# Relation adjacency built with one matmul a pair into two double banks, copied in turn by ScalarE and VectorE

## The chip, the cores and the metric

One core of a Trainium2 chip runs the kernel. The metric is the device time in microseconds of one execution. TensorE (PE), VectorE (DVE), ScalarE (ACT), GpSimd (POOL) and SyncE (SP) each take their own instructions in order and meet only at semaphores.

## The reference

A graph has 6250 nodes with 128 features and 206,250 edges sorted by destination. A SAGE network of two layers and a layer norm come first. Then come three relational convolutions. For each node d, relation r (5 of them) and layer:

```
agg[d, r] = mean of h[src] over the edges (src -> d) of relation r     (0 if there are none)
out[d]    = sum over r of agg[d, r] @ W[r]  +  h[d] @ root + bias
```

The first takes 256 inputs (128 features and a learned row for one of 3 node types) to 256, the second 256 to 128, the third 128 to 128; each ends in a ReLU. The result is added to the input of the three and normalised.

## The kernel before

**The first part (SAGE)** ends near 1488 us and is not touched, nor is its code.

**The relational convolutions** are `conv_sync`, `conv_pool`, `conv_tensor`, `conv_scalar` and `conv_vector`, one for each engine. A class `Plan` lays all of them out in half ticks. An even half tick begins with a *group*: 512 edges. POOL gathers their source rows with four indirect DMAs into one of six slots of `messages` (L1395); DVE makes one-hot columns of the destinations four groups ahead (L1669); PE multiplies rows by one-hots into one of two banks (L1408, and L1412 for the node types in the first convolution); DVE adds the bank into a ring of sums (L1690, L1691). POOL may fill a slot again when the group that used it is through PE (`group_psum`).

**Windows.** When the edges of 256 nodes (a *window*) are summed, a finish of twelve half-tick steps runs among the groups. In the first convolution: step 0, DVE scales the sums by the inverse counts (L1730), clears them (L1737) and marks node types (L1766), and SP moves the scaled type rows together with small DMAs (L1305). Step 1, PE makes the window's 256 outputs in two halves (L1495, L1496, L1493 and L1497; the last two need the DMAs' rows) into bank 4. Step 2, ACT applies bias and ReLU (L1601). Step 3, PE makes the root product of the second convolution into bank 5 (L1502) and right behind it the table product of the first 128 nodes into banks 6 and 7 (L1473). Step 4, ACT copies the root product (L1605) and the first piece of the table rows (L1582); step 5, DVE makes the residue (L1747); step 6, PE makes the second table product, which waits for that residue, and ACT and DVE go on with the pieces (L1586, L1752) to step 10. There are 25 windows.

**Building.** The second and third convolutions take the edges into the last 2688 nodes from dense matrices, source by destination, one for each relation. They are built during the first convolution: 1344 pairs of destination nodes, two pairs a *couple*, a couple each half tick, 672 couples in 20 windows. DVE makes, four pairs at a time, a one-hot of the source's lane (L1678, 128 columns) and one of the source's tile, node and relation (L1679, 490 columns). `build` (L1416) has PE multiply them for each pair. The 490 columns are cut in two slices, of 25 and 24 source tiles; slice 0 of both pairs goes to bank 2 and slice 1 to bank 3, 4 matmuls a couple. `evict` (L1548) copies them as fp8 into `stage`: ACT copies slice 0 (L1558), DVE slice 1 (L1560), of every couple. PE waits before each slice for the copy of the couple before. Eight couples fill a stage; two stages take turns, and ACT sends each to HBM with two DMAs (L1572). ACT's copy comes first in its half tick; DVE's copy of a couple comes first in the half tick after, before the one-hots of a later group, the add of a group and the scaling of a window.

The dense matmuls (L1450) of the later convolutions use banks 2 and 3 and wait at their start for the last copies.

Of the kernel before, what the change touches and what calls it, by code (L numbers as in the profile page):

```python
# [5 lines left out]
P = 128  # L6
# [4 lines left out]
RELATIONS = 5  # L11
# [165 lines left out]
def resnorm_gnn(nc, a, out):  # L177
# [27 lines left out]
    with ctx:  # L205
        sem = lambda name: ctx.enter_context(nc.semaphore(name))
        bank = [ctx.enter_context(nc.psum_tensor(f"bank{n}", [P, 512], f32)) for n in range(8)]
# [1000 lines left out]
        rel_evicted = [sem(f"rel_evicted{n}") for n in range(SLICES)]  # L1208
# [8 lines left out]
        REL_BANKS, PART_BANKS = DENSE_BANKS, TABLE_BANKS  # L1217
# [17 lines left out]
        def conv_sync(sp):  # L1235
# [62 lines left out]
            for w in range(WINDOWS_1):  # L1298
# [13 lines left out]
                if w == WINDOWS_1 - 3:  # L1312

                    sp.wait_ge(rel_hot_made, REL_BATCHES)
                    sp.wait_ge(rel_psum, COUPLES * SLICES)
# [82 lines left out]
        def conv_tensor(pe):  # L1398
# [17 lines left out]
            def build(j):  # L1416

                b, m = divmod(2 * j, BATCH)
                if m == 0:
                    pe.wait_ge(rel_hot_made, b + 1)  # L1420
                for n in range(SLICES):
                    if j:
                        pe.wait_ge(rel_evicted[n], j)
                    of_part = slice(2 * SLICE_FIRST[n], 2 * (SLICE_FIRST[n] + SLICE_TILES[n]))
                    width = 2 * SLICE_TILES[n] * RELATIONS
                    for q in range(2):
                        hot = rel_hot[:, b % 2, m + q, :].rearrange("p (r c) -> p r c", r=RELATIONS)[:, :, of_part]
                        mm = pe.matmul(bank[REL_BANKS[n]][:, q * width:(q + 1) * width], lo_dense_hot[:, b % 2, m + q, :], hot, start=True, stop=True)  # L1428
                    mm.then_inc(rel_psum, 1)

            def dense(v, step):
# [8 lines left out]
                if at == 0:  # L1440
                    if K >= 2:
                        pe.wait_ge(dense_kept, K - 1)
                    else:
                        pe.wait_ge(rel_evicted[K], COUPLES)
# [21 lines left out]
            def table(w, t):  # L1466
                n = w * WINDOW_TILES + t
                pe.wait_ge(wide_made, w + 1)
                pe.wait_ge(rest_made, ROW_SPLITS + n)
                nodes = slice(t * P, (t + 1) * P)  # L1470
                for b, cols in enumerate((slice(0, FIRST_CUT), slice(FIRST_CUT, RELATIONS * FEAT))):
                    for half in range(2):
                        mm = pe.matmul(bank[TABLE_BANKS[b]][:, 0:cols.stop - cols.start], h_wide[:, half, nodes], w2[:, half, cols], start=(half == 0), stop=(half == 1))  # L1473
                mm.then_inc(table_psum, 1)

            def finish(v, i, n):
# [4 lines left out]
                if v == 0:  # L1481
                    if n == 1:
# [3 lines left out]
                        pe.wait_ge(wide_made, w)  # L1486
                        to = [bank[WIDE_BANK][:, half * WINDOW:half * WINDOW + cols] for half in range(2)]
# [10 lines left out]
                    if n == 3:  # L1498
                        pe.wait_ge(wide_made, w + 1)
                        pe.wait_ge(root_kept, w)  # L1500
# [684 lines left out]
```

## Time and profile before

| | us |
|---|---|
| median of 3 runs | 6984.27 |
| lowest, highest | 6974.2, 6988.96 |
| profiled execution, span from first to last instruction | 7027.7 |
| PE busy, of the span | 4925.6 (70%) |
| POOL busy | 3636.8 (52%) |
| DVE busy | 2875.6 (41%) |
| ACT busy | 1023.1 (15%) |

The profiled execution has no time of its own beside its span. A line of the profile names the engine, the line of the code, the operation, what is written and read, and how often. "Idle before" is the time in which the engine stood still ahead of it, with what ended it. Starts of PE's matmuls are when they were issued; their ends are modelled. The granted clock is PE's, 1.0 for 2.4 GHz and 0.5 for 1.2 GHz.

### The profile page before, as it was taken

The numbers are of one execution on the slowest core, as the hardware profiler recorded it, in microseconds if no ns is written. First come the engines' busy times: TensorE is split into PE (matmuls) and PEld (weight loads), VectorE is DVE, ScalarE is ACT, GpSimd is POOL, SyncE is SP. The second block draws the span as 40 slices with busy tenths as digits, with TensorE's granted clock in tenths as the row PEclk, the third lists the DMA queues.
The fourth block names the chain that finished last, engine by engine and source line by source line (L and its number), as shares of the span: only waits on it lengthen the run. The fifth ranks groups of instructions, "written<-read, shape, count | busy, mean of one in ns | idle before, by whom it ended". The sixth has DMA issues, their size and how long they took to land.

```text
span 7027.7 us, 95103 instructions
## 1 busy us (share of the span) xinstructions
PE 4925.6 (70%) x35932; PEld 3076.0 (44%) x35932; DVE 2875.6 (41%) x8139; ACT 1023.1 (15%) x2385; POOL 3636.8 (52%) x3575
## 2 busy tenths in 40 slices
PE   2776789955655655656554448888888788888887
PEld 1544556633333333333333334444444445544544
DVE  5766661136666666666662211111112212111212
ACT  2544440002222222212220000000000000000000
POOL 4000000036666666666666646666666566666664
PEclk6888889977777777777776669999999899999999
DMA  2222216543434434434343334554545444444443
GB/s 77 96 111 100 90 64 227 219 135 113 121 106 120 120 105 122 119 112 117 114 116 97 97 116 134 168 167 148 169 137 167 154 138 146 138 139 147 142 135 104
DMA packets 428468, 904.12 MB, mean 129 GB/s; under 512 B 71170, under 2 KB 335116, under 8 KB 406124
## 3 DMA queue, kind: packets, MB, share of 16 engines
q0 software_dynamic: 169216, 348.44, 18.4%
q1 hardware_dynamic: 129028, 454.04, 17.7%
q10 hardware_dynamic: 129768, 95.53, 4.3%
q8 instruction: 289, 4.73, 0.3%
q14 instruction: 167, 1.37, 0.1%
HBM read 692.22 MB, written 205.05 MB: 128 GB/s over the span
## 4 chain that ended last, share of the span: by engine, by line
PE 43%; another core or an unknown queue 15%; issue 9%; DVE 8%; ACT 2%; DVEq 1%; DMA 0%; SPq 0%; ACTq 0%; POOL 0%; POOLq 0%
PE bank L1450 23%; PE bank L1408 7%; PE bank L1428 5%; PE bank L1495 2%; PE bank L1473 2%; PE bank L1412 2%; ACT stage L1558 1%; DVE stage L1560 1%; DVE scaled L1730 1%; DVE rel_hot L1679 1%; DVE type_scaled L1730 1%; DVE lo_dense_hot L1678 1%; DVE sums L1691 1%; DVE sums L1737 1%
## 5 line engine op out<-in xcount | busy, mean ns | idle before, releaser
L1395 POOL DMA_INDIRECT messages<-table,src_rows x2552 | 2653.3, 1040 | 1384.9 <-issue 692.0
L1450 PE MATMUL bank<-slices,pieces 128*128 128x384 fp8e4 x10290 | 1978.4, 337 | 375.5 <-issue 361.2
L1450 PEld LDWEIGHTS bank<-slices,pieces 128*128 128x128 bf16 x10290 | 988.8, 100 | 1211.6 <-issue 704.5
L1428 PE MATMUL bank<-rel_hot,lo_dense_hot 128*128 128x240 bf16 (+1 forms) x2688 | 589.2, 331 | 914.5 <-ACT stage L1558 463.2
L1395 POOL DMA_INDIRECT messages<-table,rel_rows x940 | 899.5, 957 | 560.8 <-issue 250.7
L1691 DVE TENSOR_TENSOR sums<-sums,bank 128x120 f32 x873 | 236.4, 271 | 2292.1 <-remote 1826.1
L1408 PE MATMUL bank<-group_hot,messages 128*128 128x120 bf16 x10476 | 832.5, 239 | 238.8 <-issue 112.8
L1408 PEld LDWEIGHTS bank<-group_hot,messages 128*128 128x128 bf16 x10476 | 747.4, 111 | 357.1 <-issue 204.8
L1428 PEld LDWEIGHTS bank<-rel_hot,lo_dense_hot 128*128 128x128 bf16 x2688 | 193.0, 106 | 1243.6 <-ACT stage L1558 532.2
L1377 POOL IOTA iota_rel_i<- 128x490 int32 x1 | 1.4, 1394 | 1355.2 <-DMA table<-typed_rows 1355.2
L1558 ACT CAST stage<-bank 128x500 fp8e4<-128x500 f32 x672 | 387.2, 576 | 1772.5 <-PE bank L1428 1094.9
L1560 DVE CAST stage<-bank 128x480 fp8e4<-128x480 f32 x672 | 435.0, 647 | 242.7 <-PE bank L1428 219.4
L877 PE MATMUL bank<-adjacency,x_pieces 128*128 128x384 bf16 (+1 forms) x2499 | 485.2, 336 | 0.0
L1679 DVE TENSOR_SCALAR rel_hot<-iota_rel,rel_dense 128x490 bf16<-128x490 f16 x1344 | 468.5, 349 | 0.0
L975 ACT CAST adjacency<-bank 128x400 bf16<-128x400 f32 x784 | 392.0, 504 | 440.4 <-PE bank L853 434.4
L1690 DVE TENSOR_TENSOR type_sums<-type_sums,bank 3x120 f32 x403 | 107.1, 266 | 812.0 <-remote 591.9
L853 PE MATMUL bank<-q_hot,lo_hot 128*128 128x100 bf16 x3136 | 230.9, 222 | 267.5 <-DVE rd_hot L1057 258.8
L877 PE MATMUL bank<-adjacency,h_pieces 128*128 128x384 bf16 (+1 forms) x2499 | 398.9, 320 | 0.0
L1678 DVE TENSOR_SCALAR lo_dense_hot<-iota,lo_dense 128x128 bf16<-128x128 f16 x1344 | 354.9, 264 | 0.0
L1669 DVE TENSOR_TENSOR group_hot<-iota,group_code 128x480 bf16<-128x480 f16 x873 | 349.5, 401 | 1.6
L853 PEld LDWEIGHTS bank<-q_hot,lo_hot 128*128 128x128 bf16 x3136 | 193.1, 105 | 344.3 <-DVE rd_hot L1057 258.7
L877 PEld LDWEIGHTS bank<-adjacency,h_pieces 128*128 128x128 bf16 x2499 | 238.5, 98 | 151.8 <-issue 3.8
(251 smaller groups left out, 3593.3 us busy)
## 6 DMA issues: line engine op xcount, KB each, us to landing
slices<-relations_d SPq DMA_DIRECT2D x70, 1200.0 KB
slices<-relations_d SPq DMA_DIRECT2D x70, 1152.0 KB
adjacency_d<-adjacency SPq DMA_DIRECT2D x15, 4704.0 KB, 14.5
adjacency<-adjacency_d SPq DMA_DIRECT2D x15, 4704.0 KB, 15.0
relations_d<-stage ACTq DMA_DIRECT2D x84, 500.0 KB
messages<-table,src_rows POOLq DMA_INDIRECT x2552
relations_d<-stage ACTq DMA_DIRECT2D x84, 480.0 KB
inverse<-inverse_d SPq DMA_DIRECT2D x52, 640.0 KB
```

The lines of the kernel that those rows point to most:

```text
L853: mm = pe.matmul(to[:, m * PAIR_COLS:(m + 1) * PAIR_COLS], lo_hot[:, i % 2, pair, :], q_hot[:, i % 2, pair, :], start=True, stop=True)
L877: mm = pe.matmul(bank[SUM_BANKS[k % 2]][:, 0:cols], pieces[:, h, piece, :], adjacency[HALF[c]][:, h, 0:cols], start=(m == 0), stop=(m == N ...
L975: act.copy(to, pairs).then_inc(evicted, 1)
L1395: pool.indirect_dma_start(messages[:, i % MESSAGES, t, 0:ROWS[v]], None, GATHERED[v], bass.IndirectOffsetOnAxis(ap=rows[:, e:e + 1], axis= ...
L1408: mm = pe.matmul(to[:, 0:GROUP_COLS], messages[:, i % MESSAGES, t, piece * P:(piece + 1) * P], group_hot[:, i % MESSAGES, t, :], start=(t ...
L1428: mm = pe.matmul(bank[REL_BANKS[n]][:, q * width:(q + 1) * width], lo_dense_hot[:, b % 2, m + q, :], hot, start=True, stop=True)
L1450: mm = pe.matmul(bank[DENSE_BANKS[K % 2]][:, 0:CHUNK], pieces[M % PIECE_RING][:, tile % PIECE_TILES, piece * P:(piece + 1) * P], slice_of_ ...
L1558: engine.copy(to, from_bank, saturate=False).then_inc(rel_evicted[n], 1)
L1560: engine.tensor_copy(to, from_bank, saturate=False).then_inc(rel_evicted[n], 1)
L1669: vec.tensor_tensor(group_hot[:, i % MESSAGES, :, :].rearrange("p k (c t) -> p k c t", t=2), iota16[:, 0:GROUP_COLS].rearrange("p (c t) -> ...
L1678: vec.tensor_scalar(lo_dense_hot[:, b % 2, m, :], iota16[:, :], lo_dense[:, b * BATCH + m:b * BATCH + m + 1], None, ALU.is_equal)
L1679: op = vec.tensor_scalar(rel_hot[:, b % 2, m, :], iota_rel[:, :], rel_dense[:, b * BATCH + m:b * BATCH + m + 1], None, ALU.is_equal)
```

## The change

- One matmul a pair now makes all 490 columns. The two pairs of a couple go to the two banks of `couple_banks[j % 2]`: banks 2 and 3 for even couples, 4 and 5 for odd ones. PE waits for the copy of the couple two before.
- A copy takes a whole couple, 980 columns out of two banks: ACT copies the even couples, DVE the odd ones. `rel_evicted` counts per engine.
- The order of the 490 columns follows the slices already in the one-hot (two iotas in place of one).
- The window product (`WIDE_1`) moves to bank 6, the root product to the first half of bank 6, the table product to bank 7 and the second half of bank 6. So the first table product moves from step 3 to step 4 and waits for ACT's copy of the root product; the window product waits for the last copies and residues of the window before.
- Waits of SP, DVE, ACT and of the first dense product follow the new counters.

```diff
-        bank = [ctx.enter_context(nc.psum_tensor(f"bank{n}", [P, 512], f32)) for n in range(8)]
+        low_banks = [ctx.enter_context(nc.psum_tensor(f"bank{n}", [P, 512], f32)) for n in range(2)]
+        couple_banks = [ctx.enter_context(nc.psum_tensor(f"couple_bank{n}", [P, 2, 512], f32)) for n in range(2)]
+        high_banks = [ctx.enter_context(nc.psum_tensor(f"bank{n}", [P, 512], f32)) for n in range(6, 8)]
+        bank = low_banks + [pair[:, n, :] for pair in couple_banks for n in range(2)] + high_banks
...
+        WIDE_1, ROOT_1 = bank[6][:, 0:2 * WINDOW], bank[6][:, 0:WINDOW]
+        TABLES_1 = (bank[7][:, 0:3 * P], bank[6][:, WINDOW:WINDOW + 2 * P])
...
-            pool.iota(iota_rel_i[:, :], [[P // 2, RELATIONS], [1, NODE_TILES], [512, 2]], base=0, channel_multiplier=0).then_inc(iota_rel_made, 1)
+            for n in range(SLICES):
+                first, width = 2 * RELATIONS * SLICE_FIRST[n], 2 * RELATIONS * SLICE_TILES[n]
+                pool.iota(iota_rel_i[:, first:first + width], [[P // 2, RELATIONS], [1, SLICE_TILES[n]], [512, 2]],
+                          base=SLICE_FIRST[n], channel_multiplier=0).then_inc(iota_rel_made, 1)
...
-                for n in range(SLICES):
-                    if j:
-                        pe.wait_ge(rel_evicted[n], j)
-                    of_part = slice(2 * SLICE_FIRST[n], 2 * (SLICE_FIRST[n] + SLICE_TILES[n]))
-                    width = 2 * SLICE_TILES[n] * RELATIONS
-                    for q in range(2):
-                        hot = rel_hot[:, b % 2, m + q, :].rearrange("p (r c) -> p r c", r=RELATIONS)[:, :, of_part]
-                        mm = pe.matmul(bank[REL_BANKS[n]][:, q * width:(q + 1) * width], lo_dense_hot[:, b % 2, m + q, :], hot, start=True, stop=True)
-                    mm.then_inc(rel_psum, 1)
+                if j >= 2:
+                    pe.wait_ge(rel_evicted[j % 2], j // 2)
+                for q in range(2):
+                    mm = pe.matmul(couple_banks[j % 2][:, q, 0:REL_COLS], lo_dense_hot[:, b % 2, m + q, :], rel_hot[:, b % 2, m + q, :], start=True, stop=True)
+                mm.then_inc(rel_psum, 1)
...
+                pe.wait_ge(root_kept, w + 1)
...
-                        pe.wait_ge(wide_made, w)
+                        pe.wait_ge(root_kept, w)
+                        pe.wait_ge(rest_made, ROW_SPLITS + w * WINDOW_TILES)
...
                         mm.then_inc(root_psum, 1)
+                    if n == 4:
                         table(w, 0)
...
-        def evict(engine, n, j):
+        def evict(engine, j):
...
-            engine.wait_ge(rel_psum, j * SLICES + n + 1)
-            if m == 0 and u >= 2:
+            engine.wait_ge(rel_psum, j + 1)
+            if m < 2 and u >= 2:
...
+            from_banks = couple_banks[j % 2][:, :, 0:REL_COLS].rearrange("p q (c d) -> p c q d", d=2)
+            to = stage[:, u % 2, :, 4 * m:4 * m + 4].rearrange("p c (q d) -> p c q d", q=2)
+            if j % 2 == 0:
+                engine.copy(to, from_banks, saturate=False).then_inc(rel_evicted[0], 1)
             else:
+                engine.tensor_copy(to, from_banks, saturate=False).then_inc(rel_evicted[1], 1)
...
-                        if 0 <= j < COUPLES:
-                            evict(act, 0, j)
+                        if 0 <= j < COUPLES and j % 2 == 0:
+                            evict(act, j)
...
-                    if v == 0 and 0 <= couple_at(half - 1) < COUPLES:
-                        evict(vec, 1, couple_at(half - 1))
+                    if v == 0 and 0 <= couple_at(half - 1) < COUPLES and couple_at(half - 1) % 2 == 1:
+                        evict(vec, couple_at(half - 1))
```

## Rows read from the trace of the kernel before

**Rows 1.** The page, part 4: shares of the chain that ended last.
```profile
PE 43%; another core or an unknown queue 15%; issue 9%; DVE 8%; ACT 2%; DVEq 1%; DMA 0%; SPq 0%; ACTq 0%; POOL 0%; POOLq 0%
```

**Rows 2.** Stretches: from:to, length, busy us (instructions) by engine, clock, DMA share, GB/s.
```profile
1488.00:3724.00 2236.00, 1302.37 (x9117) 821.95 (x9118) 1451.63 (x4643) 458.69 (x852) 1507.66 (x1381) 0.74 0.41 116
3724.00:4142.00 418.00, 176.36 (x1213) 130.10 (x1212) 102.19 (x254) 19.54 (x42) 231.18 (x232) 0.64 0.29 82
```

**Rows 3.** Waits of POOL, 1488 to 3724 us: total us, times, longest.
```profile
POOL messages L1395 <- issue: 377.5, 1236, 0.5
POOL messages L1395 <- PE bank L1412: 203.3, 64, 9.2
POOL messages L1395 <- remote: 147.6, 81, 4.4
```

**Rows 4.** Groups by form, 1488 to 3724 us: count | busy us, mean ns | idle before.
```profile
L1560 DVE CAST stage<-bank 128x480 fp8e4<-128x480 f32 x672 | 435.0, 647 | 242.7 <-PE bank L1428 219.4 <-remote 14.1 <-issue 8.7
L1558 ACT CAST stage<-bank 128x500 fp8e4<-128x500 f32 x672 | 387.2, 576 | 1772.5 <-PE bank L1428 1094.9 <-remote 632.2 <-issue 34.9
L1586 ACT CAST table_rows<-rest_w 128x640 bf16<-128x640 f32 x40 | 29.1, 728 | 3.8 <-issue 3.8
L1605 ACT ACTIVATE root_part<-bank,bias 128x256 f32<-128x256 f32 x20 | 9.6, 479 | 0.0
```

**Rows 5.** Time line, head of a window: start us, length us, engine, line, operation.
```profile
2500.43 2.37 DVE L1730 TENSOR_TENSOR scaled<-sums,inverse 128x1280 f32<-128x1280 f32 x1
...
2508.88 0.58 PE L1428 MATMUL bank<-rel_hot,lo_dense_hot 128*128 128x240 bf16 x2 [8.67 <-DVE stage L1560]
...
2514.52 0.69 PE L1493 MATMUL bank<-type_scaled,emb 18*128 18x256 f32 x2
...
2515.15 2.42 PE L1495 MATMUL bank<-scaled,w 128*128 128x256 f32 x10
...
2518.56 0.60 PE L1428 MATMUL bank<-rel_hot,lo_dense_hot 128*128 128x250 bf16 x4
...
2520.37 0.94 POOL L1395 DMA_INDIRECT messages<-table,src_rows  x1 [6.66 <-PE bank L1412]
```

**Rows 6.** Time line, tail of the same window.
```profile
2526.67 0.87 DVE L1747 TENSOR_TENSOR rest_w<-bank,table_rows 128x384 f32<-128x384 f32 x2
...
2528.16 0.58 PE L1428 MATMUL bank<-rel_hot,lo_dense_hot 128*128 128x240 bf16 x2 [0.92 <-DVE stage L1560]
...
2533.59 0.94 POOL L1395 DMA_INDIRECT messages<-table,src_rows  x1 [2.10 <-PE bank L1412]
```

**Rows 7.** Time line, head of a window with no builds in it.
```profile
3881.36 2.48 DVE L1730 TENSOR_TENSOR scaled<-sums,inverse 128x1280 f32<-128x1280 f32 x1
...
3895.07 1.21 PE L1493 MATMUL bank<-type_scaled,emb 18*128 18x256 f32 x2 [4.07 <-DMA type_scaled<-node_hot]
...
3896.21 4.45 PE L1495 MATMUL bank<-scaled,w 128*128 128x256 f32 x10
...
3903.03 0.94 POOL L1395 DMA_INDIRECT messages<-table,src_rows  x1 [4.75 <-PE bank L1412]
```

**Rows 8.** Time line, catch-up of the window of rows 5.
```profile
2563.19 0.57 ACT L1558 CAST stage<-bank 128x500 fp8e4<-128x500 f32 x1 [7.62 <-remote]
...
2563.38 0.95 POOL L1395 DMA_INDIRECT messages<-table,src_rows  x1 [1.87 <-remote]
...
2581.14 0.95 POOL L1395 DMA_INDIRECT messages<-table,src_rows  x1 [1.80 <-remote]
```

**Rows 9.** Stretches from one window's scaling to the next, with and without builds.
```profile
2610.38:2715.87 105.49, 60.70 (x434) 38.45 (x434) 69.48 (x225) 21.98 (x41) 71.71 (x66) 0.76 0.41 116
...
3881.40:3985.30 103.90, 41.65 (x304) 30.91 (x304) 23.65 (x63) 4.27 (x9) 68.08 (x68) 0.63 0.31 82
```

**Rows 10.** Stretches: second half of the window product, with and without builds.
```profile
2514.50:2518.60 4.10, 4.10 (x18) 2.82 (x18) 0.00 (x0) 0.00 (x0) 0.00 (x0) 1.00 0.06 17
...
3895.10:3900.30 5.20, 5.20 (x12) 3.74 (x13) 0.00 (x0) 0.00 (x0) 2.56 (x3) 0.50 0.30 76
```

More of the change, by code:

```diff
@@ L1442, in dense @@
                         pe.wait_ge(dense_kept, K - 1)
-                    else:
-                        pe.wait_ge(rel_evicted[K], COUPLES)
+                    elif K == 0:
+                        for n in range(2):
+                            pe.wait_ge(rel_evicted[n], COUPLES // 2)
                 if within == 0 and piece == 0:
@@ L1472, in table @@
                     for half in range(2):
-                        mm = pe.matmul(bank[TABLE_BANKS[b]][:, 0:cols.stop - cols.start], h_wide[:, half, nodes], w2[:, half, cols], start=(half == 0), stop=(half == 1))
+                        mm = pe.matmul(TABLES_1[b], h_wide[:, half, nodes], w2[:, half, cols], start=(half == 0), stop=(half == 1))
                 mm.then_inc(table_psum, 1)
@@ L1485, in finish @@
                             pe.wait_ge(emb_in, 16 * (RELATIONS + 1))
-                        pe.wait_ge(wide_made, w)
-                        to = [bank[WIDE_BANK][:, half * WINDOW:half * WINDOW + cols] for half in range(2)]
+                        pe.wait_ge(root_kept, w)
+                        pe.wait_ge(rest_made, ROW_SPLITS + w * WINDOW_TILES)
+                        to = [WIDE_1[:, half * WINDOW:half * WINDOW + cols] for half in range(2)]
                         f_cols = [slice(half * P, (half + 1) * P) for half in range(2)]
@@ L1581, in row_pieces @@
                     for b, at_r, count in ((0, 0, 3), (1, 3, 2)):
-                        op = act.copy(rows[:, at_r:at_r + count, 0, :], bank[TABLE_BANKS[b]][:, 0:count * P].rearrange("p (r f) -> p r f", f=P))
+                        op = act.copy(rows[:, at_r:at_r + count, 0, :], TABLES_1[b].rearrange("p (r f) -> p r f", f=P))
                     op.then_inc(high_made, 1)
@@ L1600, in finish @@
                         for half in range(2):
-                            op = act.activation(h_wide[:, half, 0:cols], bank[WIDE_BANK][:, half * WINDOW:half * WINDOW + cols], ACT.Relu, bias=bias[:, 2 + half:3 + half])
+                            op = act.activation(h_wide[:, half, 0:cols], WIDE_1[:, half * WINDOW:half * WINDOW + cols], ACT.Relu, bias=bias[:, 2 + half:3 + half])
                         op.then_inc(wide_made, 1)
@@ L1604, in finish @@
                         act.wait_ge(root_psum, w + 1)
-                        act.activation(root_part[:, nodes], bank[ROOT_BANK][:, 0:cols], ACT.Identity, bias=bias[:, 4:5]).then_inc(root_kept, 1)
+                        act.activation(root_part[:, nodes], ROOT_1[:, 0:cols], ACT.Identity, bias=bias[:, 4:5]).then_inc(root_kept, 1)
                         row_pieces(w, 0, 0)
```

25 lines of the change are left out of this document (9 added, 16 removed).

## The prediction

> **What bounds the kernel now.** I read the stretches first, then the waits of the gathering engine, then the time line of one window of nodes. Three relational convolutions follow a first part that ends near 1488 us. The change touches the first of them (1488 to 4142 us) and, within it, above all the 2236 us in which the dense relation matrices are built [rows 2]. PE is busy for 1302 of these 2236 us, DVE for 1452, POOL for 1508, ACT for 459 [rows 2]; no engine is full. What ends the waits is the ring of six message groups between POOL and PE. POOL issues 1381 gathers of 1507.66/1381 = 1.09 us each, and the gap that it always leaves between two of them is 377.5/1236 = 0.31 us [rows 3]; the rest of its idle time, 203.3 + 147.6 us less 145 such gaps, about 306 us, is a full ring: POOL waits for the group matmuls of PE [rows 3]. The chain of waits shows it too: PE holds 43% and an unnamed releaser 15% [rows 1]. So a us that PE saves counts only where POOL's ring is full, and at most 306 us are there to be had in this stage.
>
> Where the ring is full is seen in one window (256 nodes, 16.5 groups by the plan, about 105 us [rows 9]). Head: DVE starts to scale at 2500.43, PE is held by DVE until 2508.88, does the fp32 matmuls of the window, waits once more for a small DMA until 2514.52, and POOL gets its first free slot at 2520.37 after 6.66 us idle [rows 5]. Tail: to about 2545, POOL has gaps of its own; the one at 2533.59 is 2.10 us [rows 6]. Catch-up: for the other 60 us a cycle of 17.8 us repeats in which POOL issues 12 gathers (three groups), fills the ring, and PE, DVE, ACT and POOL resume together; ACT and POOL show it at 2563.19 and 2563.38, and the next cycle starts at 2581.14 [rows 8]. The releaser there is "remote": PE had issued its matmuls long before, and the profile doesn't say what held their marks back.
>
> The best row for this change is a stretch without any building: after 3724 us such a window takes 103.9 us, against 105.5 us with the building in it [rows 9]. It also has other DMAs, but it says that the builds are almost hidden today. POOL's mean gather there is 231.18/232 = 1.00 us against 1.09 [rows 2]: of the difference between stages a good part is DVE's one-hots slowing POOL, and those stay.
>
> **The change part by part.** Counts: 672 couples, two of them a group, in 20 windows; 5 more windows have no builds.
>
> Build matmuls: four of 250 or 240 columns (and four weight loads) become two of 490. The columns streamed are the same 980. A row of four at full clock spans 0.60 us [rows 5], latency of the last included. Two weight loads fewer save nothing if they overlap and at most 2 x 0.1 us a couple, 0.4 us of PE a group, 134 us in 336 groups; hidden behind POOL's 5 us a group (4 x 1.25) except in head and tail. I take 0 here and count it in the tail.
>
> Evictions: ACT copies 500 elements in 576 ns and DVE 480 in 647 ns for each couple [rows 4]; after it each takes 980 elements of every second couple. ACT has also 640 elements in 728 ns, a slope of (728 - 576)/140 = 1.09 ns an element; so 728 + 340 x 1.09 = 1.10 us for 980 on ACT, and 647 + 500 x 1.09 = 1.19 us on DVE. Bounds: DVE in proportion, 647 x 980/480 = 1.32 us; below, no cheaper than 0.9 us. A group costs DVE 1.19 instead of 2 x 0.647 = 1.29 us, minus 0.1 us x 336 = -34 us of DVE time, ACT 1.10 instead of 1.15. Neither is on the path in the catch-up. At the head one eviction stood right before the scaling and is now ACT's: -0.65 us a window (0 to -0.65), x 20 = -13 us. What stands between the source's two banks costs nothing in my sum; were it 0.3 us a copy, DVE would be where it is now.
> The Trainium skill says (VectorE: DVE Perf Modes, "The TRN2 errata") that VectorE and ScalarE pay a fixed part per instruction, once for a large one: by its table 980 elements from PSUM are an estimated 1.15 us on VectorE and 0.96 us on ScalarE. The sum would be within 10 us of mine.
>
> Two sets of banks, head: PE's build no longer waits for the eviction that DVE makes after its scaling. PE waited 8.67 us for it [rows 5]. Now PE can start the window's matmuls when the scaling is done, near 2505, some 4 us sooner. But the second half of these needs type rows that go through a DMA after DVE's scaling, 14.1 us after the scaling began (2514.52 - 2500.43), 13.7 in the window without builds (3895.07 - 3881.36) [rows 5, 7]. So what is late next is that DMA: the gain is its remaining wait, about 0.4 us. And there is a price. With builds, PE runs from 2508.88 into the wait, hardly pauses, and the second half has clock 1.00: ten matmuls in 2.42 us [rows 5, 10]. Without builds PE starts early, stands still for 4.07 us, and the second half has 0.50: the same ten take 4.45 us [rows 7, 10]. From scaling to POOL's first free slot it is 19.9 us with and 21.7 us without builds [rows 5, 7]. I take +2.0 us for the lost clock in nine windows out of ten, less 0.4: +1.4 us x 20 = +28 us; bounds -0.4 (the clock holds) to +2.5.
>
> Two sets, tail: PE waits in its builds for DVE (0.92 us at 2528.16 [rows 6]) and again at three more builds before 2545. They go, and POOL's gaps there shrink. Floor: in the tail POOL waits beyond its usual gaps for about 3.4 us; all of it gone is -3.4, and nothing gained 0. The second table product needs DVE's residue (0.87 us from 2526.67 [rows 6]) in any case, and that is ready only about 1 us before it is used today. I take -1.5 us x 20 = -30 us.
>
> Shared bank: the root product, its copy by ACT (0.48 us [rows 4]), then the table product, where it used to follow directly; one build now stands between, about 0.45 us, and covers most. ACT's copy is behind its eviction of the even couple (1.10 us), which has the root product's 1.0 us as cover. Behind PE's wait stand a table product, the next group and POOL. 0.1 to 0.8 us; I take 0.3 x 25 windows = +8 us. The window product's new waits are for things done 60 us earlier: 0.
>
> Catch-up: three groups in 17.8 us, 5.93 us a group, of which 4 x (0.95 + 0.30) = 5.0 is POOL's own [rows 8]. With two sets PE can issue one build and one group more before it blocks. If this makes a cycle of four groups with today's gap of 1.87 us, it is 5.5 to 5.8 us; if the gap grows as it does without builds, no gain or 0.2 us loss. About 11 groups a window x 20 = 220 groups: bounds -90 to +45 us. No row decides; I take 0.
>
> The stage stores wait for both counters and for the same eight couples: 0. DVE can now also wait for a store (second couple of a stage), but ACT's waits are at full rings and not for stores: 0. Two iotas instead of one, before the first gather: under 1 us. In the later convolutions only the first dense product's wait changes: 0.
>
> Sum: -13 + 28 - 30 + 8 + 0 = -7 us on a profiled span of 7027.7 us, which is 43 us (0.6%) above the median of the runs, 6984.3; the terms are carried over as they are, and rounded: 6980 us.
>
> **Rivals.** (a) The clock. The head's loss is full and the tail gives little: +2.5 x 20 = +50, -0.5 x 20 = -10, shared bank +0.5 x 25 = +12, DVE -13, say +40 us: 7024 us. For it: all windows without builds have the slow second half. Against: PE has a build and a group just before. It decides from the point where the head's +1.9 us is more than eviction and tail bring (2.15 us a window).
> The Trainium skill (TensorE: Matmul & The Clock Gate, "HAM oscillation") speaks against this change with the same rule: an array left idle is throttled to half its clock and what follows starts cold. The rows on the second half agree with it (1.00 against 0.50).
> (b) The ring gains. Run-ahead makes cycles of four groups, clock or not: 220 x -0.25 = -55, tail -40, +10 for the rest: 6984 - 85 = 6900 us. For it: PE and ACT wait for each other's single set in every active cycle. Against: these cycles end with POOL's ring, not with PE's work, and 103.9 us without any build is no better than this.
> (c) The change doesn't do what it says: copies across two banks take 1.32 us or more and PE waits for DVE as before, with a build that now needs a whole couple copied. DVE is busy 1452 of 2236 us; 0.3 us x 336 = 100 us more of it, a third of it seen: 7015 us.
>
> **How the numbers follow.** My case (gain and loss cancel) 0.36, the clock 0.26, the ring 0.28, the copies 0.10. A run tells about 0.2%, 14 us, from no change. My case reaches from 6955 to 7000 us: 0.08 of it faster by more, 0.28 same. So faster 0.08 + 0.28 = 0.36, same 0.28 + 0.02 = 0.30, slower 0.24 + 0.10 = 0.34. The range for 8 in 10 goes from the ring's case to the clock's with some of their own spread: 6890 to 7035; my own case's range is 6955 to 7000.
>
> **What would show it.** Right: DVE copies of 128x980 near 1.19 us, ACT's near 1.10; PE's wait for DVE's eviction at the head gone and a wait for the type rows of some 4 us there; granted clock 0.5 in the second half of the window matmuls; POOL's first free slot 20 to 22 us after the scaling; stage length 2236 us within 30. Wrong: second halves at 1.00 (then -30 to -50 us more), cycles of other than 12 gathers, POOL's waits for PE's groups far from 350 us, a mean gather that leaves 1.09 us.

## The result and the profile after

The changed kernel takes 6933.88 us (median of 8 runs, 6914.56 to 6947.71), the kernel before, beside it, 6975.67 us (8 runs, 6953.44 to 6988.96): ratio 0.9941, 95% interval 0.9929 to 0.9953, 42 us or 0.6% faster. The time lies in my range, but that range is wide enough to hold the times of all three rivals too; my likeliest case was no measurable change (6980 us), and it came out on the side of rival (b).

The profiled execution of after has a span of 6929.0 us. Its page, first the busy time, then the chain of waits (answers to [rows 1]), then groups of instructions:

```profile
PE 4825.4 (70%) x34588; PEld 2947.4 (43%) x34588; DVE 2832.1 (41%) x7803; ACT 972.3 (14%) x2049; POOL 3715.9 (54%) x3576
...
PE 34%; another core or an unknown queue 14%; DVE 14%; issue 10%; DVEq 1%; SPq 1%; DMA 1%; POOL 1%; ACT 1%; ACTq 0%; POOLq 0%
...
L1432 PE MATMUL couple_bank<-rel_hot,lo_dense_hot 128*128 128x490 bf16 x1344 | 475.1, 450 | 678.8 <-DVE rel_hot L1685 367.9
...
L1564 ACT CAST stage<-couple_bank 128x980 fp8e4<-128x980 f32 x336 | 327.7, 975 | 1359.9 <-remote 697.2
...
L1566 DVE CAST stage<-couple_bank 128x980 fp8e4<-128x980 f32 x336 | 389.9, 1160 | 232.5 <-PE couple_bank L1432 192.3
```

PE has gone from 43% of the chain to 34%, DVE has 14%, and what PE's builds wait for most is no longer a copy but DVE's one-hots. Stretches of after (columns as in [rows 2]); the second has the same limits as the first of [rows 2]:

```profile
1488.00:3724.00 2236.00, 1238.13 (x7904) 717.54 (x7904) 1418.27 (x4331) 407.66 (x516) 1596.33 (x1417) 0.74 0.42 119
3724.00:4083.00 359.00, 164.94 (x1080) 119.65 (x1080) 95.81 (x229) 19.54 (x42) 198.78 (x196) 0.64 0.28 80
4083.00:6929.00 2846.00, 2299.31 (x16280) 1368.29 (x16280) 524.03 (x1399) 42.14 (x105) 1836.49 (x1880) 0.95 0.48 150
```

In the same 2236 us POOL gets 1417 instructions done instead of 1381. The first gather of the second convolution comes at 4083 us; it was at 4142 in before. The later convolutions, in which nothing but one wait was changed, take 2846 us here and 2885 in the profiled execution of before, though both do 16280 matmuls:

```profile
4142.00:7027.00 2885.00, 2328.46 (x16280) 1385.00 (x16280) 526.68 (x1399) 42.14 (x105) 1813.99 (x1880) 0.94 0.47 148
```

These 39 us are not the change's. The profiled before is 52 us over its median. The same two lengths come back in the experiments: 2881 to 2888 us in all profiles of e1 to e8, where before had medians of 7031 and 7036 us, and 2845 to 2855 in those of e9 to e12, where it had 6978. I don't know the cause (e1 to e4 and e9 to e12 ran on the same chip), so of profiles only the first convolution is compared below. Even there a single profile is good to some 15 us only: the first gather of the second convolution comes 59 us earlier in after's profile, though the timed difference is 42 us, and in e9, the same kernel profiled again, it comes at 4092 us and not at 4083.

**Where the 48 us of the windows with builds came from.** POOL's time can be split without a rest. From the first window's scaling to the scaling of the window after the last build (1636.7 to 3779.1 us in before, 2142.4 us; 1634.6 to 3728.9 in after, 2094.3 us) POOL does nothing but gathers. The stretch restricted to the gathers, before and then after:

```profile
1636.70:3779.10 2142.40, 1440.74 (x1316) 0.74 0.40 115
```
```profile
1634.60:3728.90 2094.30, 1494.05 (x1318) 0.74 0.42 118
```

And POOL's waits in it (us in total, times, longest), before and then after:

```profile
POOL messages L1395 <- issue: 359.3, 1175, 0.6
POOL messages L1395 <- PE bank L1412: 200.7, 63, 9.2
POOL messages L1395 <- remote: 141.9, 78, 3.9
```
```profile
POOL messages L1403 <- issue: 376.8, 1236, 0.4
POOL messages L1403 <- PE bank L1420: 132.6, 41, 11.4
POOL messages L1403 <- remote: 91.2, 41, 3.5
```

The gaps that POOL always leaves are 400 us in both. Full rings, less such a gap of 0.305 us each: before 200.7 + 141.9 - 141 x 0.305 = 299.6 us, after 132.6 + 91.2 - 82 x 0.305 = 198.8 us. So the stops fell by 101 us, and 53 us of that were given back at once: about as many gathers took 1494 us instead of 1441, 1.134 us each instead of 1.095. That is the whole account: -101 + 53 = -48. The second profile of after (e9 in the table) gives -88 + 52, with 3 us more in the usual gaps, and comes out 32 us shorter than before. Beside DVE's `rel_hot` one-hots lies most of the added gather time: put down to the DVE instruction that covers most of a gather, the time over 0.946 us beside them rose from 68 to 122 us, with about the same 442 and 434 us of such instructions (my own sum over the trace). A gather beside them took 1.13 us in before and 1.30 in after, one with DVE idle 0.95 and 0.96. The five windows without builds and what follows them up to the second convolution are also 9 us shorter in after (364 and 354 us; e9 351), which I can't explain.

**The head of a window**, after (answers to [rows 5]):

```profile
2478.28 2.35 DVE L1736 TENSOR_TENSOR scaled<-sums,inverse 128x1280 f32<-128x1280 f32 x1
...
2483.01 4.63 PE L1502 MATMUL bank<-scaled,w 128*128 128x256 f32 x10 [4.36 <-DVE type_scaled L1736]
...
2491.40 1.21 PE L1500 MATMUL bank<-type_scaled,emb 18*128 18x256 f32 x2 [3.32 <-DMA type_scaled<-node_hot]
2492.55 4.63 PE L1502 MATMUL bank<-scaled,w 128*128 128x256 f32 x10
...
2500.31 1.24 POOL L1403 DMA_INDIRECT messages<-table,src_rows  x1 [11.39 <-PE bank L1420]
```
```profile
2483.00:2487.50 4.50, 4.49 (x11) 3.59 (x12) 3.97 (x6) 0.00 (x0) 3.58 (x4) 0.50 0.26 64
2487.60:2491.30 3.70, 0.48 (x3) 0.08 (x1) 1.99 (x10) 0.00 (x0) 1.02 (x1) 0.95 0.23 60
2492.60:2497.20 4.60, 4.60 (x12) 3.70 (x12) 0.00 (x0) 0.00 (x0) 0.00 (x0) 0.50 0.00 0
```

The wait for DVE's copy is gone, the one for the type rows has come, and both halves of the product run at clock 0.50 (1.2 GHz), ten matmuls in 4.63 us each. For the second half that is new: it took 2.42 us at 1.00 [rows 5, 10]. Between the halves the clock had risen (0.95 over 2487.6 to 2491.3 us), but PE was busy for only 0.48 of those 3.7 us, and it fell again. POOL starts again 22.0 us after the scaling, where it was 19.9. This head stands for the others: in all 20 windows with builds PE waits 2.9 to 4.4 us for the type rows, and the second half takes 3.8 to 4.6 us, against 2.42 or 2.43 in all 20 of before.

**The catch-up**, after: in the window that begins at 2580.6, these two are the only gaps of POOL over the usual 0.30 us from 2610 us to its end at 2683:

```profile
2615.88 0.95 POOL L1403 DMA_INDIRECT messages<-table,src_rows  x1 [1.10 <-remote]
...
2669.78 0.95 POOL L1403 DMA_INDIRECT messages<-table,src_rows  x1 [3.51 <-remote]
```

POOL runs for 50 us between the two stops. Before, there was such a stop every 17.8 us, after 12 gathers [rows 8]. Over the 20 windows, from 45 us after each scaling, before has 72 stops, 53 of them after 12 gathers; after has 25, most of them after 24 to 36 gathers (e9: 35).

### The profile page after: what moved, and what is told of

It reads as the page before. It is cut to its first block, busy times and chain, and to the rows that moved or that the text cites. A ratio compares the mean times of both kernels' runs of the same rounds, so it can differ in the third digit from the quotient of the medians.

```text
span 6929.0 us, 91721 instructions
## 1 busy us (share of the span) xinstructions
PE 4825.4 (70%) x34588; PEld 2947.4 (43%) x34588; DVE 2832.1 (41%) x7803; ACT 972.3 (14%) x2049; POOL 3715.9 (54%) x3576
## 4 chain that ended last, share of the span: by engine, by line
PE 34%; another core or an unknown queue 14%; DVE 14%; issue 10%; DVEq 1%; SPq 1%; DMA 1%; POOL 1%; ACT 1%; ACTq 0%; POOLq 0%
PE couple_bank L1455 21%; PE bank L1416 5%; DVE rel_hot L1685 3%; DVE lo_dense_hot L1684 2%; DVE stage L1566 2%; PE bank L1479 2%; PE bank L1502 2%; DVE group_hot L1675 1%; PE couple_bank L1432 1%; DVE scaled L1736 1%; SPq L1310 1%; DVE sums L1697 1%; POOL messages L1403 1%; DVEq L1690 1%
## 5 line engine op out<-in xcount | busy, mean ns | idle before, releaser
L1455 PE MATMUL couple_bank<-slices,pieces 128*128 128x384 fp8e4 x10290 | 1942.7, 333 | 304.0 <-issue 296.8
L1455 PEld LDWEIGHTS couple_bank<-slices,pieces 128*128 128x128 bf16 x10290 | 982.4, 99 | 1118.3 <-issue 598.2
L1432 PE MATMUL couple_bank<-rel_hot,lo_dense_hot 128*128 128x490 bf16 x1344 | 475.1, 450 | 678.8 <-DVE rel_hot L1685 367.9
L1564 ACT CAST stage<-couple_bank 128x980 fp8e4<-128x980 f32 x336 | 327.7, 975 | 1359.9 <-remote 697.2
L880 PE MATMUL couple_bank<-adjacency,x_pieces 128*128 128x384 bf16 (+1 forms) x2499 | 486.1, 337 | 0.0
L1566 DVE CAST stage<-couple_bank 128x980 fp8e4<-128x980 f32 x336 | 389.9, 1160 | 232.5 <-PE couple_bank L1432 192.3
L880 PE MATMUL couple_bank<-adjacency,h_pieces 128*128 128x384 bf16 (+1 forms) x2499 | 398.9, 320 | 0.0
L880 PEld LDWEIGHTS couple_bank<-adjacency,h_pieces 128*128 128x128 bf16 x2499 | 238.5, 98 | 151.8 <-issue 3.8
L1502 PE MATMUL bank<-scaled,w 128*128 128x256 f32 (+1 forms) x500 | 216.8, 617 | 114.4 <-DVE type_scaled L1736 114.4
L1057 DVE TENSOR_TENSOR lo_hot<-iota,lo_code 128x1024 bf16<-128x1024 f16 x392 | 266.6, 680 | 46.4 <-PE bank L858 28.2
```

The costliest lines, as they stand in the source:

```text
L880: mm = pe.matmul(bank[SUM_BANKS[k % 2]][:, 0:cols], pieces[:, h, piece, :], adjacency[HALF[c]][:, h, 0:cols], start=(m == 0), stop=(m == N ...
L1432: mm = pe.matmul(couple_banks[j % 2][:, q, 0:REL_COLS], lo_dense_hot[:, b % 2, m + q, :], rel_hot[:, b % 2, m + q, :], start=True, stop=True)
L1455: mm = pe.matmul(bank[DENSE_BANKS[K % 2]][:, 0:CHUNK], pieces[M % PIECE_RING][:, tile % PIECE_TILES, piece * P:(piece + 1) * P], slice_of_ ...
L1502: pe.matmul(to[half], w1[:, r, f_cols[half]], scaled[:, r, 0:cols], start=(r == 0), stop=False)
L1564: engine.copy(to, from_banks, saturate=False).then_inc(rel_evicted[0], 1)
L1566: engine.tensor_copy(to, from_banks, saturate=False).then_inc(rel_evicted[1], 1)
```

## The experiments

Theory A: the gain is PE's run-ahead over two sets, which keeps the ring from filling. Theory B: it is the smaller number of matmuls and copies. The experiments were timed in three groups, e1 to e4, e5 to e8 and e9 to e12, each group side by side with the kernel before. Ratios are to before within the group, with 95% intervals. "Stops" are full rings as worked out above, "gathers" their total, both over the windows with builds, from one profile each. Two profiles of one kernel, after and e9, differ by 16 us in the windows and by 13 in the stops, so smaller differences in these columns tell nothing.

| kernel | us | ratio | windows | stops | gathers |
|---|---|---|---|---|---|
| before (profile) | | | 2142.4 | 299.6 | 1440.7 |
| after (profile) | | | 2094.3 | 198.8 | 1494.1 |
| e1 one set's depth | 7030.67 | 0.9999 (0.9989-1.0010) | 2138.9 | 291.4 | 1446.4 |
| e2 two sets, a pair an engine | 7101.10 | 1.0089 (1.0069-1.0109) | 2218.0 | 314.5 | 1501.3 |
| e3 one set, a pair an engine | 7132.23 | 1.0144 (1.0129-1.0160) | 2246.7 | 428.9 | 1416.8 |
| e4 shared bank alone | 7022.35 | 0.9994 (0.9982-1.0007) | 2134.5 | 318.8 | 1414.0 |
| e5 two sets alone | 7050.58 | 1.0018 (1.0009-1.0027) | 2170.0 | 272.7 | 1494.0 |
| e6 product in two banks | 6962.32 | 0.9888 (0.9873-0.9904) | 2093.1 | 191.2 | 1496.5 |
| e7 four matmuls | 7039.14 | 1.0011 (0.9998-1.0024) | 2155.3 | 252.2 | 1501.3 |
| e8 PE kept busy | 7039.10 | 1.0002 (0.9991-1.0014) | 2165.1 | 254.2 | 1508.0 |
| e9 after again | 6933.77 | 0.9940 (0.9922-0.9959) | 2110.2 | 212.1 | 1492.7 |
| e10 all copies on ACT | 6951.97 | 0.9971 (0.9953-0.9989) | 2103.8 | 219.3 | 1481.0 |
| e11 e10 with e6 | 6925.32 | 0.9930 (0.9913-0.9946) | 2080.6 | 177.3 | 1500.7 |
| e12 e6's edit in before | 6952.89 | 0.9966 (0.9954-0.9977) | 2134.8 | 320.0 | 1413.4 |

Before had 7031.24 us beside e1 to e4, 7035.92 beside e5 to e8 and 6978.03 beside e9 to e12.

**e1, one set's depth**

```
-                if j >= 2:
-                    pe.wait_ge(rel_evicted[j % 2], j // 2)
+                if j >= 1:
+                    pe.wait_ge(rel_evicted[(j - 1) % 2], (j - 1) // 2 + 1)
```

> The kernel after, except that TensorE waits at every couple for the copy of the couple just before it, so that the second set of banks never lets it run ahead; copies in turn, one matmul a pair and the shared bank stay. Theory A (the gain of 41 us is TensorE's run-ahead over two sets, which keeps the ring of six groups from filling): the gain is gone, 6965 to 6995 us, ratio to before 0.999 to 1.003, and the catch-up shows a full ring about every 12 gathers again. Theory B (the gain is fewer instructions: half the matmul instructions and half the copies, the depth has nothing to do with it): 6925 to 6945 us, ratio 0.993 to 0.996. Theory C (the gain is that VectorE has no copy ahead of the scaling and of the groups' one-hots): as B here, since the turns stay.

0.9999: with one set's depth and all else as after there is no gain, as A has it; B alone is out. The stops don't come back in the old pattern of 12 gathers: from 45 us after each scaling there are 74, mostly after 8, 12 or 16. PE's waits in its builds, from 1636 to 3660 us, in after and then in e1:

```profile
PE couple_bank L1432 <- DVE rel_hot L1685: 321.6, 133, 11.9
...
PE couple_bank L1432 <- DVE stage L1566: 92.7, 143, 3.3
...
PE couple_bank L1432 <- ACT stage L1564: 72.5, 14, 11.1
```
```profile
PE couple_bank L1432 <- ACT stage L1564: 433.7, 185, 10.7
...
PE couple_bank L1432 <- DVE stage L1566: 203.4, 97, 9.0
```

Waits for copies are 637 us in e1, as long as in before (627), and 165 in after. The stops are back at 291 us, the gathers back at 1446.

**e2 and e3, both engines copy, one pair each** (e3 waits for couple j - 1, e2 for j - 2)

```
-            from_banks = couple_banks[j % 2][:, :, 0:REL_COLS]...
-            to = stage[:, u % 2, :, 4 * m:4 * m + 4]...
+            from_bank = couple_banks[j % 2][:, q, 0:REL_COLS].rearrange("p (c d) -> p c d", d=2)
+            to = stage[:, u % 2, :, 4 * m + 2 * q:4 * m + 2 * q + 2]
```

> The kernel after, except that each couple's two pairs are copied by the two engines at once, ScalarE the bank of the first, VectorE that of the second (490 columns each); TensorE still runs two sets ahead. Theory A (run-ahead of TensorE): most of the gain stays, 6930 to 6955 us; VectorE's copy comes back ahead of each window's scaling (some 0.65 us a window, 16 us) and its copies cost more in all (336 more instructions). Theory B (fewer instructions of the copies): most of the gain goes, 6955 to 6985 us. Theory C (VectorE has no copy ahead of the scaling): 6945 to 6965 us, and TensorE waits for VectorE's copy at the head of each window again.

> The kernel before with one matmul a pair and the shared bank: both engines copy one pair of each couple and TensorE waits for both copies of the couple just before, so the depth is one set, as before. Theory A (run-ahead of TensorE): 6965 to 6990 us, ratio to before 0.998 to 1.002; the window's product waits at its head for VectorE's copy as before. Theory B (half the matmul instructions on TensorE, whatever the copies): 6935 to 6955 us. Against the kernel with two sets and the same copies, theory A has this one 20 to 40 us slower, theory B has both equal.

Both missed, for a reason that I hadn't priced. ACT's and DVE's copies in e2:

```profile
L1565 ACT CAST stage<-couple_bank 128x490 fp8e4<-128x490 f32 x652 | 776.0, 1225 | 1344.0 <-PE couple_bank L1433 858.6 <-remote 420.4 <-issue 58.3
...
L1567 DVE CAST stage<-couple_bank 128x490 fp8e4<-128x490 f32 x652 | 767.9, 1178 | 191.5 <-PE couple_bank L1433 162.6 <-remote 28.6
```

490 elements written two bytes at a time take 1225 and 1178 ns; the 500 and 480 of before, four bytes at a time, took 576 and 647 [rows 4]. The order in which PSUM is read changed with it, and no run takes the two apart. So these two tell nothing on the copies in turn. They still differ from each other in depth alone, and were timed side by side: 31 us between the medians (intervals 1.0069 to 1.0109 and 1.0129 to 1.0160), 29 between the windows, and 114 us between the stops, of which the gathers took back 85. It is the cleanest pair on what the second set is worth, though with slow copies.

**e4, the shared bank alone** (the kernel before; window product, root part and second table piece in one bank, the table a step later)

> The kernel before with one part of the change alone: the window's product, its root part and the second piece of the table rows share a bank, and the first table is built a step later. My working put +8 us on it (+0.3 us a window). Theories A, B and C all expect 6970 to 6995 us, no gain. Rival D (the layout of the banks, with ScalarE and VectorE reading other banks than TensorE writes, is where the gain comes from): 6935 to 6960 us.

0.9994 (0.9982 to 1.0007), against my +8 us: no cost to be seen, and no gain from the layout.

**e5, two sets alone** (copies by slices, as in before, four matmuls)

```
+                for n in range(SLICES):
+                    first, width = 2 * RELATIONS * SLICE_FIRST[n], 2 * RELATIONS * SLICE_TILES[n]
+                    for q in range(2):
+                        mm = pe.matmul(couple_banks[j % 2][:, n, q * width:(q + 1) * width], ...
```

> The kernel before with two sets of banks alone (and the shared bank that makes room for them): four matmuls a couple into banks by slices, ScalarE copying 500 and VectorE 480 columns of every couple at once, as before, but TensorE waits for the couple two back. Theory A (run-ahead alone makes the gain): ratio to before 0.992 to 0.997, on the order of the whole change's 0.994. Theory B' (run-ahead pays only with the cheaper steps: half the matmul instructions, no VectorE copy ahead of the scaling): 0.998 to 1.003, and with this the ring fills about as often as before. Under A the catch-up shows one or two full rings a window instead of four.

1.0018, where B' expected no gain: depth alone is worth nothing here, and A is not enough. The stops fell only to 272.7 us, the gathers rose by all of the 53 us. Beside e4, which is before with the shared bank, it is 46 us of stops less and 80 us of gathers more. One thing besides the depth differs from before: both copies wait for all four matmuls of a couple, where slice 0 could be copied after two.

**e6, the window's product in two banks**

```
+        WIDE_HALVES = (bank[6][:, 0:WINDOW], bank[7][:, 0:WINDOW])
...
+                        pe.wait_ge(typed_in, 16 * (RELATIONS + 1) * (w + 1))
+                        for half in range(2):
+                            mm = pe.matmul(to[half], emb_all[:, f_cols[half]], typed_all[:, 0:cols], start=False, stop=True)
+                        mm.then_inc(window_psum, 1)
```

> The kernel after, but the window's product has its two halves in two banks, so that all twelve matmuls of it that do not need the type rows come before the wait for them, and only the two short ones with the type rows behind it. If TensorE's wait at the head (3.3 to 4.4 us, with the second half of the product at the half clock behind it) lies on the path: 5 us less at each head from the scaling to the end of the product, the first gather of the ring 3 to 5 us earlier in each window, 60 to 100 us less in all, ratio 0.980 to 0.987. If the head is given back in the catch-up (the gathers, not TensorE, set the window's length): under 20 us, ratio 0.991 to 0.995.

0.9888 (0.9873 to 0.9904), the lowest ratio of all, between the two expectations. Time line of a head:

```profile
2472.50 2.37 DVE L1736 TENSOR_TENSOR scaled<-sums,inverse 128x1280 f32<-128x1280 f32 x1
...
2477.31 4.48 PE L1499 MATMUL bank<-scaled,w 128*128 128x256 f32 x10 [4.25 <-issue]
...
2482.05 2.32 PE L1499 MATMUL bank<-scaled,w 128*128 128x256 f32 x10
...
2485.70 1.13 PE L1503 MATMUL bank<-type_scaled,emb 18*128 18x256 f32 x4 [0.89 <-DMA type_scaled<-node_hot]
...
2488.55 1.24 POOL L1404 DMA_INDIRECT messages<-table,src_rows  x1 [4.90 <-PE bank L1421]
```

PE works through the time in which it stood still, the second half is at full speed, and POOL starts 16.0 us after the scaling instead of 22.0 (a median of 17.4 over the windows, against 22.2 in after). But an earlier start is not a saved stop: at the heads (14 to 32 us after a scaling) the stops fell from 111 to 78 us beside after, and elsewhere they rose from 88 to 114, so that the windows with builds are as long as in after's profile, 2093.1 us, and 17 us shorter than in e9's.

**e7, four matmuls a couple** (250 and 240 columns of each pair; all else as after)

> The kernel after, but each pair's matmul of 490 columns is split into one of 250 and one of 240, so that a couple has four matmuls again; everything else stays. Theory A (run-ahead): ratio 0.994 to 0.997, as after or a little above, since four took 2.42 against two some 0.9 to 1.0 us at the ends, mostly hidden. Theory B (the number of matmul instructions): the gain goes, 0.998 to 1.002.

1.0011, in the range of theory B, so the number of matmuls matters too. The stops are 252.2 us, halfway back, the gathers as long as in after. The builds' busy time hardly moved (493.8 us for 2672 matmuls against 475.1 for 1344), 19 us more where I had put the most at 134; PE's waits for the copies rose from 165 to 278 us. By which way two more matmuls a couple do this stays open.

**e8, PE kept busy to the type rows** (24 matmul instructions more, whose product is used nowhere)

> The kernel after, with twelve matmuls more in each window's product, into a bank that nobody reads, between its first half and the wait for the type rows: work that computes nothing and only keeps TensorE busy through the wait. Priced in my working: the second half of the product took 4.45 us at half clock against 2.42 at full, 2.0 us a window. If that is the loss and it lies on the path: the second half takes 2.4 to 2.6 us again, 20 windows x 2 = 40 us less, ratio 0.988 to 0.990. If the twelve outlast the wait (12 x 0.24 = 2.9 us at full clock against a wait of 3.3 to 4.4, longer at a lower clock), they give it back: 0.993 to 0.996.

```profile
2512.06 5.34 PE L1500 MATMUL bank<-scaled,w 128*128 128x256 f32 x24
2517.33 0.69 PE L1502 MATMUL bank<-type_scaled,emb 18*128 18x256 f32 x2
2517.96 2.43 PE L1504 MATMUL bank<-scaled,w 128*128 128x256 f32 x10
```
```profile
2518.00:2521.00 3.00, 3.00 (x14) 2.41 (x14) 0.00 (x0) 0.00 (x0) 0.00 (x0) 1.00 0.00 0
```

Adding work does hold the clock: granted clock 1.00, 2.43 us again instead of 4.63, and POOL starts 20 to 22 us after the scaling. But the ratio is 1.0002, above both expectations. I had priced the twelve at 2.9 us; each is two instructions in the profile, the 24 took 5.34 us, and the product comes to the type rows about 1 us after they are there. The windows are 2165.1 us long and the stops 254.2 us, both well above after's. So e8 shows that the clock can be had back and that this way of it gains nothing. It does not show what the slow clock alone costs, since the added work has a price of its own.

**e9, after again**

> The kernel after itself, beside the kernel before on this chip: on the chip of the first comparison its ratio was 0.994, and four edits of it measured since on another (one set's depth, four matmuls, twelve matmuls added) all had 1.000 to 1.001, so a reader must know what the whole change is worth where they were measured. If the gain does not hang on the chip: 0.992 to 0.996, and each of these edits takes it away. If it does: 0.998 to 1.001, and the edits then show nothing.

0.9940, as in the first comparison. But before was back at 6978 us, so the condition in which e1 to e8 ran, with before at 7031 and 7036 us, was still not tested with after itself.

**e10, all copies on ACT**

```
-            if j % 2 == 0:
-                engine.copy(to, from_banks, saturate=False).then_inc(rel_evicted[0], 1)
-            else:
-                engine.tensor_copy(to, from_banks, saturate=False).then_inc(rel_evicted[1], 1)
+            engine.copy(to, from_banks, saturate=False).then_inc(rel_evicted[j % 2], 1)
```

> The kernel after, but ScalarE copies every couple (980 columns) and VectorE none. From the trace of after: VectorE is freed of 336 x 1160 ns = 390 us, 17 us a window, and ScalarE takes 336 x 975 ns = 328 us more. Theory V (with two sets the windows are set by VectorE: TensorE's largest wait is for the relation one-hots of VectorE, and gathers lose 12 us a window beside it): 30 to 80 us less than after, ratio to before 0.982 to 0.990. Rival S (a couple in flight on ScalarE alone takes 975 ns and both sets hang on one engine, which also has the window's activations and table rows ahead of it, so TensorE waits there): as before or slower, 0.998 to 1.005.

0.9971, between the two expectations and slower than after's 0.9940 beside it, with barely touching intervals. From 1488 to 3724 us DVE is busy for 362 us less than in e9 (1057.42 against 1419.65) and nothing comes of it:

```profile
1488.00:3724.00 2236.00, 1205.05 (x7888) 727.99 (x7888) 1057.42 (x3992) 710.77 (x852) 1578.15 (x1412) 0.74 0.41 118
```

So the sum of DVE's work doesn't bound the windows, and it isn't DVE's copies that lengthen the gathers (1.120 us each without them, 1.123 in e9). Nor did PE wait longer for copies, as S had it (89 us from 1636 to 3660 us, 125 in e9); why e10 is slower than after stays open.

**e11 and e12, the two banks of e6 with e10, and in the kernel before**

> Both edits at once: ScalarE copies every couple, and the window's product stands in two banks with only two matmuls behind the type rows. The halves alone had 0.989. If the gains of the head and of VectorE's relief add up: 0.972 to 0.982. If they are the same gain taken twice (each shortens the wait that fills or empties the ring): 0.984 to 0.989.

> The kernel before with the window's product in two banks and only two of its matmuls behind the wait for the type rows; one set's depth, four matmuls a couple and the shared copies stay. In before the first wait of the product was for VectorE's copy (8.67 us in the row of the head) and the type rows were there when TensorE came to them in most windows, so theory P (the head is cured only where the early wait for VectorE's copy is gone): 0.996 to 1.001. Rival Q (the halves gain by themselves, whatever the depth): 0.985 to 0.993, as much as they gained over after.

e11 has 0.9930, above both of its expectations, 27 us under e10 beside it; e12 has 0.9966, 25 us under before beside it. The edit is thus worth about 25 us in either of these kernels. In e12 PE still waits for DVE's copy:

```profile
2506.59 0.58 PE L1429 MATMUL bank<-rel_hot,lo_dense_hot 128*128 128x240 bf16 x2 [8.26 <-DVE stage L1561]
```

The ratio lies at P's edge, but P expected no gain, and 25 us is clear of none; Q's range is missed as well. The windows with builds are as long as in e4 (2134.8 against 2134.5 us); most of what e12 gains it gains in the five windows without builds, where PE always came early. From the scaling of the first of these to the first gather of the second convolution it takes 340.5 us, e4 364.4:

```profile
3772.10:4112.60 340.50, 154.64 (x1048) 116.07 (x1048) 92.94 (x218) 19.42 (x42) 193.28 (x195) 0.65 0.29 84
```
```profile
3770.40:4134.80 364.40, 160.55 (x1048) 116.42 (x1048) 93.06 (x218) 19.53 (x42) 193.13 (x193) 0.64 0.27 78
```

By these single profiles P's reasoning held for the windows it spoke of, and I had overlooked the others. e11 is the fastest kernel of its group and e6 has the lowest ratio; the two were not timed beside each other. By ratio e6 is clear of after's interval, though in another group, and e11 is not.

## Why the time was right and the mechanism was not

The range held the time because it reached from the ring's case to the clock's, and my own case was a sum of -7 us in which terms with wrong signs cancelled. The measured 6934 us lies outside the 6955 to 7000 of that case. That the wide range held it is luck, not a mechanism that held. Three of my own signs of being wrong came true: the stops were no longer 12 gathers apart, POOL's waits for PE's groups fell from 351 to 231 us over the 2236 us [rows 3], and the mean gather left 1.09 us for 1.13.

- **The term that failed** is "Catch-up: ... No row decides; I take 0". From 45 us after each scaling POOL's stops fell from 112 to 64 us (78 in e9). The mechanism stood there as rival (b), run-ahead by one build and one group. I gave it cycles of four groups instead of three; most stops now come after six to nine. e1, where the second set gives no run-ahead, has 121 us there. My reason for 0, that the cycles end with POOL's ring and not with PE's work, took the ring for the cause where it was largely the effect: in before PE waits 627 us for copies, and with the second set these waits are 165 us and the ring is full less often.
- **A second sign was wrong: the head**, +28 us. Each observation was right: the wait for the type rows (3.3 us above), the clock at 0.50 in the second half, POOL's first free slot 22.0 us after the scaling. But POOL's stops at the heads (14 to 32 us after a scaling) fell from 151 to 111 us. A later restart costs only from the moment that POOL stands still, and after a catch-up with fewer stops POOL may stop later; that this is why they fell is argued, not shown. I had taken a delay of PE for a stop of POOL. e6 agrees from the other side: it restarts POOL some 5 us earlier than after, 95 us over 20 windows, and shortens the windows with builds by only 1 to 17 us; its edit was worth about 25 us by time in before and in e10.
- **The tail** was over-sized: -30 us forecast, and between 32 and 45 us after the scaling the stops fell from 39 to 25 us, so -14.
- **What I left out: the gathers.** I wrote that DVE's one-hots slow POOL "and those stay". The mean of 1.09 us became 1.13, +53 us, half of what the ring gave. It is more than the difference between rival (b)'s 84 us and the 42 measured. e10 excludes DVE's copies as the cause.
- **Copies**: 1.19 and 1.10 us forecast for 980 elements, 1.160 and 0.975 measured. DVE's is near, ACT's 13% too high: my slope of 1.09 ns an element was too steep for ACT, which added 0.83 from 500 to 980. Rival (c) is out. The Trainium skill (VectorE: DVE Perf Modes, "The TRN2 errata") has a table by which the estimate was 1.15 and 0.96 us; the trace agrees within 2%.
- **Build matmuls**: taken as 0. With four instead of two (e7) the gain is gone, so in this kernel they are a condition of it; the run-ahead with four matmuls and the copies by slices (e5) has 1.0018.
- **Shared bank**: +8 us forecast, 0.9994 measured (e4), so -4 us with 9 either way.
- **The clock** (rival (a)) does fall as I wrote, in every window rather than in nine of ten: PE stands still for 3.3 us and what follows has clock 0.50. By the Trainium skill (TensorE: Matmul & The Clock Gate, "HAM oscillation") the array is throttled while it waits for data and the next work starts at the lower clock; the trace agrees. It did not make the kernel slower than before; what it still costs inside after no run isolates.

What stays open: e1, e5, e7 and e8 were timed without after beside them, while before and they had some 50 us more than in the groups with after. That after would have had 0.994 there wasn't measured. Three things speak for it: e6, which is after with one edit, was timed beside e7 and e8 and has 0.9888 where they have 1.0011 and 1.0002, and its edit was worth only 0.4% in the two other kernels; e2 and e3 differ in depth alone, side by side; and the stops of e1, e5, e7 and e8 say that each loses part of what after gains. So "both depth and fewer matmuls are needed" is well supported and not settled. It would take after, e1 and e7 side by side. Also open is why the gathers beside the one-hots lengthen with two sets, and why two more matmuls a couple cost so much.

## What to carry to other kernels

Where a full ring between two engines shows a regular pattern of stops, try depth on the consumer's side before judging that its other work is "almost hidden": a wait of the consumer is hidden only until the ring is full. Count the producer's time whole (its instructions, its usual gaps, its stops): here half of what the stops gave was lost in longer gathers, which no single wait shows. And a delay at one place is worth what it adds to the producer's stops, not its own length: some 5 us at each of 20 heads (e6 against after) came to at most 17 us of the windows with builds.

## What the hardware showed unexpectedly

- A copy from PSUM to fp8 written in runs of two bytes took about twice as long as one written in runs of four: 1225 against 576 ns on ACT, 1178 against 647 on DVE, with about as many elements (e2, [rows 4]). The order of reading differed too.
- POOL's indirect gathers are longer beside DVE's `rel_hot` one-hots: 1.30 us in after, against 0.96 with DVE idle. Beside its copies of 980 elements from PSUM they are hardly so: without these copies the gathers still had 1.120 us on average (e10), against 1.123 (e9).
- The same matmuls of the later convolutions took 2845 to 2855 or 2881 to 2888 us, and both lengths came up on one chip (e9 to e12, e1 to e4), with granted clocks of 0.95 and 0.94 in the stretches shown. The cause is open.
